# Output projections of the first self attention from split factors, with the split of the divided output on GpSimd and ScalarE

## The reference

```
xq, xk, xv = x @ wq.T, x @ wk.T, x @ wv.T            # x (4, 1024, 256), w (1024, 256)
xq, xk, xv = (t.reshape(4, 16, 1024, 64) for t in (xq, xk, xv))
out  = softmax(xq @ xk^T * 64**-0.5) @ xv            # per batch and head
y    = out.reshape(4, 1024, 1024) @ wo.T             # wo (256, 1024)
x    = layernorm(x + y)
```

## Time and profile before

| | before |
|---|---|
| median of 3 runs | 2905.53 us |
| profiled execution, time / span | 2910.15 us / 2908.4 us |
| TensorE busy (matmul) | 2539.5 us, 87% |
| VectorE busy | 1822.7 us, 63% |
| ScalarE busy | 1578.1 us, 54% |
| GpSimd busy | 1621.8 us, 56% |
| mean granted TensorE clock | 0.936 |

### The profile page before, as it was taken

The page is one execution under the profiler, slowest core; times in us unless marked ns, Lnnn a source line. Parts: engine busy times, 40 slices in busy tenths (PEclk is TensorE's granted clock), DMA queues, the critical chain, the costliest instruction groups (busy, mean ns, idle before and its releaser), DMA issues. The chain is left out here.

```text
span 2908.4 us, 43888 instructions
## 1 busy us (share of the span) xinstructions
PE 2539.5 (87%) x12067; PEld 1413.8 (49%) x12067; DVE 1822.7 (63%) x3044; ACT 1578.1 (54%) x2568; POOL 1621.8 (56%) x1344
## 2 busy tenths in 40 slices
PE   6999999999999999999999959971994687798695
PEld 4555555555555555555554434540673344454264
DVE  4677777777777777777777636661334555478733
ACT  4676666766666676666666625540222343354234
POOL 2677677777767777776777733425335114333343
PEclk8999999999999999999999989985996798899698
DMA  7454454555445455544443230003992100000232
GB/s 185 123 130 119 122 129 121 134 128 130 119 122 129 121 133 128 130 120 122 130 121 104 57 92 2 2 31 126 378 347 78 27 0 1 31 2 12 69 110 88
DMA packets 413441, 309.49 MB, mean 106 GB/s; under 512 B 296950, under 2 KB 341406, under 8 KB 408350
## 3 DMA queue, kind: packets, MB, share of 16 engines
q1 hardware_dynamic: 397118, 238.27, 31.6%
q0 software_dynamic: 12272, 63.92, 6.2%
q10 hardware_dynamic: 3952, 6.08, 0.6%
HBM read 193.33 MB, written 94.13 MB: 99 GB/s over the span
## 5 line engine op out<-in xcount | busy, mean ns | idle before, releaser
L757 POOL TENSOR_TENSOR a_total<-a_total,a_pr 128x1024 f32<-128x1024 f32 x384 | 916.0, 2385 | 277.0 <-ACT a_pr L742 259.2
L626 DVE TENSOR_REDUCE a_nmax<-a_psX 128x1 f32<-128x1024 f32 x512 | 624.1, 1219 | 280.2 <-PE a_psX L619 280.2
L742 ACT ACTIVATE a_pr<-a_psS 128x1024 f32<-128x1024 f32 x512 | 496.5, 1022 | 369.9 <-PE a_psS L729 351.9
L771 PE MATMUL a_psO<-a_pr,a_vd 128*64 128x512 f32 x2048 | 492.5, 602 | 0.0
L723 PE MATMUL a_psS<-a_qA,a_kA 128*128 128x512 f32 x1024 | 292.1, 406 | 8.2 <-DVE a_psS L680 4.4
L618 PE MATMUL a_psX<-a_kA,a_qA 64*128 64x512 f32 x512 | 233.8, 457 | 29.3 <-DVE a_nmax L626 25.8
L757 POOL TENSOR_TENSOR a_total<-a_pr 128x1024 f32<-128x1024 f32 x64 | 152.0, 2375 | 192.5 <-ACT a_pr L742 192.5
L771 PEld LDWEIGHTS a_psO<-a_pr,a_vd 128*64 128x64 f32 x2048 | 129.9, 136 | 242.0 <-issue 240.6
L696 DVE COPY a_psS<-a_least 128x1024 f32<-128x1024 f32 x192 | 232.7, 1212 | 4.6 <-ACT a_pr L742 4.6
L619 PE MATMUL a_psX<-a_kB,a_qA 64*128 64x512 f32 x512 | 233.9, 457 | 0.0
L635 ACT ACTIVATE a_diag<-a_ident,a_nmax 128x128 fp32r<-128x128 f32 x512 | 186.1, 401 | 83.0 <-DVE a_nmax L626 83.0
(11 more groups left out here) (423 smaller groups left out, 4884.9 us busy)
## 6 DMA issues: line engine op xcount, KB each, us to landing
a_qA<-a_qhi SPq DMA_DIRECT2D x248, 128.0 KB
a_qB<-a_qlo SPq DMA_DIRECT2D x124, 256.0 KB
a_vd<-a_vg SPq DMA_DIRECT2D x128, 128.0 KB
a_kA<-a_khi SPq DMA_DIRECT2D x124, 128.0 KB
a_kA<-a_klo SPq DMA_DIRECT2D x62, 256.0 KB
a_qhi<-a_ph SPq DMA_DIRECT2D x120, 128.0 KB
a_qlo<-a_pl SPq DMA_DIRECT2D x120, 128.0 KB
a_khi<-a_ph SPq DMA_DIRECT2D x120, 128.0 KB
```

Of the source, the lines that this page charges most:

```text
L626: w.eng.tensor_reduce(nmax[:, u:u + 1], psX[:, :, :].rearrange("p a k -> p (a k)"), AX.X, ALU.max, negate=True)\
L742: w.eng.activation(pr[:, n, :], both(psS[:, i % 2, :, :]), ACT.Exp, scale=SCALE).then_inc(sems["e"], 1)
L757: w.eng.tensor_tensor(total[:, buf, :], first, pr[:, n, :], ALU.add).then_inc(sems["ad"], 1)
L771: last = w.eng.matmul(psO[q * HD:(q + 1) * HD, :], vd[:, b, kc, :], pr[:, n, q * 512:(q + 1) * 512], start=p == 0 and i == 0, stop=p == KC ...
```

## The change

The eight float32 products of an output projection become 24 float32r products: `oh*woh`, `oh*wol`, `ol*woh`. `divide` becomes three steps for each head: GpSimd multiplies `oU` with `rec` in place (semaphore `dq`), ScalarE rounds the result into the chunks of `oh` (semaphore `oh`), GpSimd subtracts `oh` from it and writes `ol` (semaphore `ot`). The weight wo is loaded into `vg` and split once in the prologue, before the fifth key piece; the first evacuations into `vg` wait for that. What else the diff holds are names and semaphores.

```diff
-        wo = m.sb("wo", [P, KC, D])
+        woh, wol = (m.sb(n, [P, KC, D], F32R) for n in ("woh", "wol"))
...
                 elif kind == "O":
-                    w.wait("w", 16)
+                    w.wait("wl", 4)
                     w.wait("ot", w.at("ot"))
-                    for c in range(KC):
-                        last = w.eng.matmul(ps[:, 0:D], oT[:, buf, c, :], wo[:, c, :], start=c == 0, stop=c == KC - 1)
+                    for n, (op, wp) in enumerate(((oh, woh), (oh, wol), (ol, woh))):
+                        for c in range(KC):
+                            last = w.eng.matmul(ps[:, 0:D], op[:, buf, c, :], wp[:, c, :],
+                                                start=n == 0 and c == 0, stop=n == 2 and c == KC - 1)
...
         def divide(w, j):
+            def chunks(t):
+                return t[:, j // 2, :, (j % 2) * HD:(j % 2 + 1) * HD]
+
+            whole = oU[:, :].rearrange("p (c t) -> p c t", t=HD)
             if w.on("gpsimd"):
                 w.wait("nm", w.at("nm"))
                 w.wait("rec", w.at("rec"))
-                w.eng.tensor_tensor(oT[:, j // 2, :, (j % 2) * HD:(j % 2 + 1) * HD],
-                                    oU[:, :].rearrange("p (c t) -> p c t", t=HD),
-                                    rec[:, :].rearrange("p (c t) -> p c t", t=HD), ALU.mult).then_inc(sems["ot"], 1)
+                w.eng.tensor_tensor(oU[:, :], oU[:, :], rec[:, :], ALU.mult).then_inc(sems["dq"], 1)
+            w.inc("dq")
+            if w.on("scalar"):
+                w.wait("dq", w.at("dq"))
+                w.eng.activation(chunks(oh), whole, ACT.Copy).then_inc(sems["oh"], 1)
+            w.inc("oh")
+            if w.on("gpsimd"):
+                w.wait("dq", w.at("dq"))
+                w.wait("oh", w.at("oh"))
+                w.eng.tensor_tensor(chunks(ol), whole, chunks(oh).bitcast(F32), ALU.subtract).then_inc(sems["ot"], 1)
             w.inc("ot")
...
             for i in range(2 * KC):
-                if i in (3, KC):
-                    split((3, KC).index(i) + 1)
+                if i in (3, KC, KC + 4):
+                    split((3, KC, KC + 4).index(i) + 1)
```

More of the change, by code:

```diff
@@ L353, in layer0_self_attention @@
         inv = m.sb("inv", [P, 512 // 32])
-        oT = m.sb("oT", [P, 2, KC, P])
+        oh, ol = (m.sb(n, [P, 2, KC, P], F32R) for n in ("oh", "ol"))
         res = m.sb("res", [P, 2, D])
@@ L368, in layer0_self_attention @@
         names = ("cst", "cstv", "wq", "wk", "wv", "w", "x", "mi", "md", "ma", "xl", "wh", "wl", "ch", "a0", "a1", "q0", "q1", "b0", "b1", "fa0", "fa1", "fb0", "fb1", "sg", "sh", "bv", "mx", "mxr", "dg", "bc", "sv", "sa", "lv", "la", "s", "e",
-                 "ad", "pv", "nm", "rec", "ot", "var", "pl", "rstd", "y", "yo", "dv")
+                 "ad", "pv", "nm", "rec", "dq", "oh", "ot", "var", "pl", "rstd", "y", "yo", "dv")
         sems = {n: m.sem(n) for n in names + tuple(f"so{n}" for n in range(PIECES))}
@@ L480, in misc @@
                     w.wait("bv", w.at("bv"))
+                    if not out:
+                        w.wait("wl", 4)
                     w.wait("mi", w.at("mi"))
@@ L886, in split @@
             def split(n):
-                hi, lo, full = ((wqh, wql, pr[:, 0:2, :]), (wkh, wkl, pr[:, 2:4, :]), (wvh, wvl, total[:, :, :]))[n]
+                hi, lo, full = ((wqh, wql, pr[:, 0:2, :]), (wkh, wkl, pr[:, 2:4, :]), (wvh, wvl, total[:, :, :]),
+                                (woh, wol, vg[:, :, :].rearrange("p a (c e) -> p (a c) e", e=D)))[n]
                 if w.on("scalar"):
-                    w.wait(("wq", "wk", "wv")[n], 16)
+                    w.wait(("wq", "wk", "wv", "w")[n], 16)
                     w.eng.activation(hi[:, :, :], full, ACT.Copy).then_inc(sems["wh"], 1)
@@ L963, in _ @@
                 eng.dma_start(t, src.rearrange("(a p) o -> p a o", p=P)).then_inc(sems[n], 16)
-            eng.dma_start(wo[:, :, :], woT.rearrange("(c p) e -> p c e", p=P)).then_inc(sems["w"], 16)
+            eng.dma_start(vg[:, :, :].rearrange("p a (c e) -> p (a c) e", e=D), woT.rearrange("(c p) e -> p c e", p=P))\
+                .then_inc(sems["w"], 16)
             eng.preload_act_table(ACT.Exp)
```

## The result

The changed kernel takes 3178.5 us (median of 6 runs, 3176.87 to 3190.95) against 2905.43 us of the kernel before on the same chip: 273.1 us more, a ratio of 1.0945 with a 95% interval of 1.0933 to 1.0957. The forecast was 3204, so 26 us too high. The profiled execution has a span of 3176.2 us.

A forecast was written before the change was run, and what follows sets the result against it. TensorE was taken to bound the kernel. From the profiled 2910.15: - 24.6 (products) + 217.8 (waits) + 100.6 (clock) + 2.3 (prologue) + 2.1 (epilogue) = 3208.4; the median lies 4.6 lower, so 3204 us, range 3100 to 3275.

The forecast's parts named there:

- TensorE sets the pace: First self attention: TensorE is busy 1501.89 of 1543 us, so its work saved is time saved unless it newly waits.
- The saving: Output projections: 24 products at 0.12 us take 2.88 in place of 3.65 us, 24.6 us less over 32.
- The new wait: Each head: ScalarE's rounding waits for GpSimd's product, delaying TensorE's last `largest` by 2.93 or, with normalization, 4.26 us; 217.8 in all.
- The last six heads: No projection piece in pass 2, so only exponentials delay the weighted sums: 1.6 us, or 2.9 with normalization, three heads each.
- The root ahead of the product: Heads with normalization: GpSimd does four small operations before the division's product, which starts 1.33 us later in the head.
- VectorE held by `pl`: Pass 2: VectorE's `pl` waits for ScalarE's `ph`, so the reduction behind it ends 3.4 us late, holding TensorE's last `largest`.
- The rival without it: Only the exponentials delay the sums in all heads: stall 141 in place of 217.8 us, time 3111 us; chance 0.06.
- The clock: TensorE's clock falls after the new rest in every head, costing 1.4 us (short rests) or 1.8 (long), 100.6 us in all.
- The next head's loads: SyncE sends the pass 2 piece 3 to 4 us later, but the loads behind it have a whole head of lead.
- The prologue: VectorE gets one more operation of 2.28 us ahead of the first head's transfers: +2.3 us, bounds 0 and 4.6.
- The epilogue: Rounding, remainder and two signals join the chain: 0.60 + 1.28 + 0.2 = +2.1 us.
- The rest unchanged: The cross attention and what follows it should take as long as before.

The follow-up runs named there:

- products_only: The changed kernel without the remainder: GpSimd writes the rounded quotient in one operation, the 24 products and the weight split stay; 2882.5 us, ratio 0.9925.
- piece_first: The changed kernel with ScalarE making `ph`, its copy of the projection piece, ahead of the rounding; 3059.99 us, ratio 1.0535.
- root_behind: The changed kernel with GpSimd's four short operations of the normalization's root moved behind the division's product; 3118.6 us, ratio 1.0735.
- zero_fewer: The changed kernel with 11 or, with normalization, 16 products of a zero tile in TensorE's rest ahead of the last maxima; 3120.19 us, ratio 1.0739.
- round_late: The changed kernel with rounding and remainder later, rounding before pass 3's exponentials or at the head's end, quotient kept in `rec`; 2889.35 us, ratio 0.9947.
- all_gpsimd: The changed kernel with all three division steps on GpSimd: rounded quotient, quotient into `rec`, remainder; 2893.84 us, ratio 0.9953.

## Why the prediction was right, step by step

- **TensorE sets the pace, and work saved there is time saved:** right; `products_only` shows it by itself.
- **The saving, 0.77 us each, 24.6 in all:** over by a fifth. A projection fell from 3.65 to 3.01 us, 0.64 less, so 32 give some 20; the 63 heads of `products_only` are 21.8 us shorter. The pace of 0.12 us came from the earlier trace rows, where six pairs of float32r products, not six products, take 1.44 us; 24 in a row took 0.125 each. The rule that I set against it (the Trainium skill, FP8 and Floating Point Precision, TensorE Precision Notes: four passes for a true float32 product) would have 3.65 fall by a quarter to 2.74. The trace agrees in part: one of the eight float32 products (two instructions in the trace) took 0.456 us, 3.6 times a float32r product and not 4, so it fell by 18%. The row was the nearer of the two (0.77) and still too kind.
- **The new wait, 2.93 us without normalization and 4.26 with it:** the mechanism is right at every link, in the order in which the prediction lists them. The size is 0.1 us over in each head, for TensorE rested 2.80 and 4.10 where 2.9 and 4.2 were expected. The signals were too long in my sum: from the product's end to the rounding it was 0.03 us (1037.26 to 1037.29) and not 0.1. The sum of 217.8 measured 207.4. The last six heads are in it with 13.5 us and rested 13.3 ahead of the weighted sums.
- **The root ahead of the product as the reason for 1.33 us more:** right, and by experiment: without it all rests are 2.8.
- **VectorE held by `pl`:** right. The rival without it had 141 in place of 217.8 us of stall, 77 less; `piece_first` had 78.7 less.
- **The clock, 100.6 us:** right in kind and near in sum (88.3), but put together wrongly. I expected a fall in every head at 1.4 to 1.8 us; there were 46 in 63 heads, at 1.9. The two errors cancel in part, so that the sum came so near is partly luck.
- **The next head's loads, nothing:** right for the change, which never waits for them, but with less to spare than a whole head of lead suggests: its relatives wait for these transfers for 7.1 us (`root_behind`) to 11.7 us (`zero_fewer`) in all.
- **The prologue, +2.3:** measured 2.45.
- **The epilogue, +2.1:** measured -2.0. The added step itself is as forecast: from the start of GpSimd's product to the projection 3.47 us in place of 1.41, 2.06 more. But that product starts 5.55 us behind the last copy and not 8.74, because in the slower last heads GpSimd is less far behind with its sums (TensorE's products of L441 wait 1.70 us for them, not 5.58). I had taken the state in which the last head leaves GpSimd as unchanged.
- **The rest unchanged:** 5.4 us less. 4.6 of that I had put down to the profiled execution of before, which was that much above its median.

The sum of 3208.4 against 3178.2 of the profiled execution is thus 10.4 from the waits, 12.3 from the clock, 4.1 from the epilogue and 5.4 from the rest, less 3 to 4 from the projections (24.6 against 20 to 21.8); the parts leave 1 to 2 us unassigned.

## What to carry to other kernels

Before an operation that waits for another engine is put into an engine's order, look at what stands behind it in that order, and at what stands behind those on the engines that they feed: here a ScalarE operation of 0.63 us a head, waiting for GpSimd's product, cost 296 us over the same products without it, and placed later 7 at most, as far as two chips can be compared. Where the waiting operation's own result is needed much later than its place, move it towards its user (`round_late`), or let the engine that makes its input make it as well (`all_gpsimd`). And count a rest on a dense TensorE at more than its length: here 207 us of rests brought 88 more.

## What was not expected of the hardware

- Rests of the same 2.80 us were followed by a fall of the clock in about half the cases (17 of 31 in the change, 32 of 58 in `root_behind`) and not in the other half, and those of 4.1 us always (29 of 29).
- Products of zeros keep the granted clock at 1.00 as well as real ones. At 0.25 us each for 512 columns (212.0 us for 853) they only pay where the time is otherwise lost: they took the rest's place and gave back 58 us.
- The first, second and third eight float32r products of the projection at 1048.90 take 1.06, 0.95 and 1.04 us from start to start.
- GpSimd writes the rounded float32r quotient in 1278 ns, as fast as the float32 one (1277), from `all_gpsimd`:

```profile
L808 POOL TENSOR_TENSOR a_oh<-a_oU,a_rec 128x512 fp32r<-128x512 f32 x64 | 81.8, 1278 | 4.1 <-DVE a_rec L795 4.1
L813 POOL TENSOR_TENSOR a_rec<-a_oU,a_rec 128x512 f32<-128x512 f32 x64 | 81.7, 1277 | 5.0
```
